# Edge softmax of a graph layer: indirect gathers spaced by clearings on GpSimd in place of waits on TensorE

## The chip, the core and the metric

The kernel runs on one core of a Trainium2 chip. The metric is device time in microseconds of one execution. Engines are named as in the profile: PE is TensorE (matmuls; PEld its weight loads), DVE is VectorE, ACT is ScalarE, POOL is GpSimd, SP is SyncE, which here only issues DMAs.

## The reference, cut to what matters

The kernel is a whole model of four layers on 16384 tokens of 64 channels. The change touches one stage of the third layer's feed-forward part: a graph attention over 262144 edges (and a loop at each node) that yields gate scores for four experts.

```python
h = (x_flat @ W_gat).reshape(M, HEADS, NUM_EXPERTS)        # M = 16384 nodes, 4 heads, 4 experts
a_src = (h * att_src).sum(-1)
a_dst = (h * att_dst).sum(-1)
e = leaky_relu(a_src[src] + a_dst[dst], negative_slope=0.2)
e_max = segment_max(e, dst, num_segments=M)
ee = jnp.exp(e - e_max[dst])
denom = segment_sum(ee, dst, num_segments=M)
alpha = ee / (denom[dst] + 1e-16)
msg = h[src] * alpha[:, :, None]
agg = segment_sum(msg, dst, num_segments=M).reshape(M, 16) + b_gat
```

What costs time in it is `h[src]` and `a_src[src]`: for each edge the row of its source node, 16 values and 4 logits.

## The kernel before, in words

The edges are sorted by destination and lie as 128 lanes of 2048 edges. `edge_softmax` (L3266) goes over them in 32 chunks of 64 columns; a column is 128 edges, one per lane. The source rows of the 64 columns of a chunk come in two ways:

- **34 columns by DMA** (`BY_DMA`): GpSimd issues one indirect gather per column (L3373), which reads 128 rows of 20 words from a table in HBM into `rows[:, k, c]`. `rows` is double: chunk n uses slot k = n mod 2.
- **30 columns on TensorE** (`ON_PE`, six groups of five): SyncE loads node places (`lanes`, L3326), VectorE compares them with node numbers to make one-hot matrices (`hot`, L3482, four instructions per group), TensorE multiplies these with the node table in two parts (L3391, eight matmuls of 128x512 per column into one of five PSUM banks), ScalarE copies each bank out (L3412), and VectorE picks one of 32 rows by the low bits of the number (`select`, L3497 to L3504).

VectorE then works through a chunk c: `logits` (L3510 to L3522), `maxima` (L3527 to L3539), `sums` (L3543 to L3548); ScalarE does the exponentials and turns the results round for the store. The order on VectorE is written out: during the six groups of chunk c+1 it does `logits(c)` behind group 0, `maxima(c)` behind group 1 and `sums(c)` at group 3.

What orders the gathers of chunk n:

- `idx_ready`: the column indices of chunk n are copied by VectorE in `maxima(n-2)` (L3468), behind its wait for the gathers of chunk n-2.
- `rows_used`: `sums(n-2)` (L3546) has read slot k for the last time. The first two chunks find both set ahead.
- `bank_full`, the pacing: gather c of chunk n waits until TensorE has filled a number of columns, `banks_before + c * ON_PE // BY_DMA`, so that 34 gathers go along with 30 columns. In the loop `banks_before` is `n * ON_PE - PACE_BEHIND`, ten columns early. The first two chunks stand ahead of the loop, with numbers of their own. Only c = 0 has no such wait.

The reader of the gathers of chunk n is `maxima(n)`: a wait on `gathered[k]` at L3527, behind which come L3468 (not in the last two chunks), L3531 and L3533. `wait_apart` (L36) is a wait followed by an increment of a semaphore that nobody waits for.

Of the kernel before, what the change touches and what calls it, by code (L numbers as in the profile page):

```python
# [10 lines left out]
BF16 = mybir.dt.bfloat16  # L11
# [8 lines left out]
P = 128  # L20
# [15 lines left out]
def wait_apart(eng, sem, value, passed):  # L36


    eng.wait_ge(sem, value)
    eng.sem_inc(passed, 1)  # L40
# [2855 lines left out]
HEADS2, CH = 4, 16  # L2896
# [170 lines left out]
GROUPS, PER_GROUP = 6, 5  # L3067
ON_PE = GROUPS * PER_GROUP
BY_DMA = CHUNK - ON_PE
# [2 lines left out]
LOW_PLACES = TILES // BLOCKS  # L3072
LOW_BITS = LOW_PLACES.bit_length() - 1
HOT_COLUMNS = CHUNKS * ON_PE
PACE_BEHIND = 2 * PER_GROUP


class HotPlaces:
# [187 lines left out]
def edge_softmax(nc, g, q, att_src):  # L3266

    C, W = CHUNK, CHUNK + 1
    NI = CHUNKS // 2
# [4 lines left out]
    with Stage(nc, "edges") as st:  # L3274
# [1 line left out]
        idx = st.sb("idx", [P, 2, C], I32)  # L3276
        inp_s, acc_s, decay = (st.sb(n, [P, HEADS2, 1 + PERH, W]) for n in ("inp_s", "acc_s", "decay"))
        lanes = st.sb("lanes", [P, LANE_SLOTS, PER_GROUP, P], F16)
        att = st.sb("att", [P, CH])
        nodes_i, nodes = st.sb("nodes_i", [P, BLOCKS], I32), st.sb("nodes", [P, BLOCKS])  # L3280
        pow2 = st.sb("pow2", [P, LOW_BITS], I32)
        tabs_p, weights_p, dst_p = (st.ps(n, [P, 512]) for n in ("tabs_p", "weights_p", "dst_p"))
# [22 lines left out]
        (split, numbered, powers, att_in, hot_ready, bank_full, fetched_in, halved, selected, pe_passed, act_passed, dve_passed, bits_ready) = (  # L3305
            st.sem(n) for n in ("split", "numbered", "powers", "att_in", "hot_ready", "bank_full", "fetched_in", "halved", "selected",
                                "pe_passed", "act_passed", "dve_passed", "bits_ready"))
        cleared, own, idx_ready, rows_used, passed, diff_ready, exped, sums_ready, state_ready, starts_used = (
            st.sem(n) for n in ("cleared", "vec_own", "idx_ready", "rows_used", "pool_passed", "diff_ready", "exped",
                                "sums_ready", "state_ready", "starts_used"))  # L3310
# [2 lines left out]
        with nc.Block() as block:  # L3313
# [47 lines left out]
            @block.gpsimd  # L3361
            def _(pool):
                nc.gpsimd.iota(nodes_i[:], pattern=[[1, BLOCKS]], base=0, channel_multiplier=BLOCKS).then_inc(numbered, 1)
                for s in range(LOW_BITS):
                    nc.gpsimd.memset(pow2[:, s:s + 1], LOW >> (s + 1)).then_inc(powers, 1)

                def gather(n, k, banks_before):
                    pool.wait_ge(idx_ready, n + 1)
                    wait_apart(pool, rows_used, n + 1, passed)
                    for c in range(BY_DMA):  # L3370
                        if c:
                            wait_apart(pool, bank_full, banks_before + c * ON_PE // BY_DMA, passed)
                        nc.gpsimd.indirect_dma_start(  # L3373
                            out=rows[:, k, c, :], out_offset=None, in_=q.t_table,
                            in_offset=bass.IndirectOffsetOnAxis(ap=idx[:, k, c:c + 1], axis=0)).then_inc(gathered[k], 16)

                gather(0, 0, 1)
                gather(1, 1, ON_PE - 4)
                with pool.Fori(1, NI) as i:
                    for k in range(2):  # L3380
                        gather(2 * i + k, k, (2 * i + k) * ON_PE - PACE_BEHIND)

            @block.tensor
            def _(pe):
# [415 lines left out]
def ffn2(nc, g, q, I):  # L3800

    turned_norm(nc, g, "ln_f2", g.H, known=True)
    with Stage(nc, "expc_in") as kept:
        tables = ExpertTables(nc, kept, I["L2_ffn_W1"], I["L2_ffn_W2"], I["L2_ffn_b1"], I["L2_ffn_b2"])
        with ExitStack() as ctx:
            q.tables(nc, ctx)
            node_logits(nc, g, q, I["L2_ffn_W_gat"], I["L2_ffn_att_src"], I["L2_ffn_att_dst"])
            edge_softmax(nc, g, q, I["L2_ffn_att_src"])
            carry_states(nc, g, q)
            node_gates(nc, g, q, I["L2_ffn_b_gat"], I["L2_ffn_ln_gamma"], I["L2_ffn_ln_beta"], ahead=tables)  # L3810
        experts(nc, g, "expc", tables, target=g.H, measure=True)
# [70 lines left out]
```

## Time and profile before

| | us |
|---|---|
| median of 3 runs | 6534.55 |
| lowest and highest run | 6527.07, 6545.31 |
| the profiled execution's own time | 6565.2 |
| its span | 6563.5 |
| edge stage in it, first gather to last store's issue | 3166.73 to 5022.19 |

| busy over the whole span | us |
|---|---|
| PE | 5217.5 (79%) |
| DVE | 4890.5 (75%) |
| ACT | 2537.8 (39%) |
| POOL | 2268.8 (35%) |

How to read it. The page is one profiled execution. A group of instructions has a line number, an engine, an operation, what it writes and reads and with which shapes, then its busy time and the mean of one in ns, then the idle time of the engine just before these instructions and what released it; "issue" means that the engine waited for nothing that the profile shows. In a timeline each row is start, duration, engine, line and operation, "x4" for four merged instructions, and in brackets the idle time before it. The table by stage gives for each stretch the busy time of each engine with its number of instructions, the granted clock of TensorE as a share of full speed, and the DMA engines' busy share. Times on POOL are rough: the duration of a gather is that of making its descriptors, not of its data's arrival.

### The profile page before, as it was taken

To read this page: it belongs to the slowest core of one execution; us is meant where nothing else is said; L and a number is where in the kernel's file an instruction comes from. 1 tells how busy PE (TensorE), PEld (TensorE's weight loads), DVE (VectorE), ACT (ScalarE), POOL (GpSimd) and SP (SyncE) were. 2 spreads that over 40 slices of the span, in tenths; PEclk is the share of its full clock that TensorE was granted. 3 is DMA by queue.
4 is the path that set the end of the run, shared out by engine and by line. 5 is a ranking of instruction groups with operands and counts; after the bars stand their busy time and mean duration, and the time that the engine had idled before them with its cause. 6 is when DMAs were issued, how large, how long until landed. Compare 5 with 4: busy or idle time off the path is not lost. (4 is left out here: it accounts for less than half of the span.)

```text
span 6563.5 us, 111024 instructions
## 1 busy us (share of the span) xinstructions
PE 5217.5 (79%) x41117; PEld 3540.3 (54%) x41184; DVE 4890.5 (75%) x8592; ACT 2537.8 (39%) x4432; POOL 2268.8 (35%) x2268
## 2 busy tenths in 40 slices
PE   6577968885469999971699999999994088967998
PEld 3462236554246666541577877778773025852452
DVE  6878988887878888870478888888886357767657
ACT  3443433333246666650233343333432043222332
POOL 0010010002223333325566666656663601014555
PEclk8778989997679999985799999999997598978999
DMA  0200000112210000001111121111111000030241
GB/s 17 78 6 1 20 23 29 35 41 65 72 32 6 6 9 11 10 10 40 22 39 40 37 41 41 41 36 41 40 40 27 8 1 3 3 65 15 68 105 33
DMA packets 241447, 206.47 MB, mean 31 GB/s; under 512 B 116682, under 2 KB 215923, under 8 KB 239251
## 3 DMA queue, kind: packets, MB, share of 16 engines
q1 hardware_dynamic: 173630, 147.27, 7.8%
q0 software_dynamic: 67408, 53.34, 5.3%
q8 instruction: 271, 4.44, 0.3%
q14 instruction: 126, 1.03, 0.1%
q10 hardware_dynamic: 12, 0.39, 0.0%
HBM read 113.55 MB, written 67.86 MB: 28 GB/s over the span
## 5 line engine op out<-in xcount | busy, mean ns | idle before, releaser
L3391 PE MATMUL edges_bank<-part_room,hot_room 128*128 128x512 f32 x7680 | 1778.8, 392 | 237.2 <-DVE hot_room L3482 190.0
L3391 PEld LDWEIGHTS edges_bank<-part_room,hot_room 128*128 128x128 f32 x7680 | 1440.3, 188 | 575.7 <-issue 253.6
L3373 POOL DMA_INDIRECT XT<-gat_node_table,edges_idx x1088 | 1113.8, 1024 | 706.4 <-issue 327.8
L3412 ACT COPY XT<-edges_bank 128x512 f32<-128x512 f32 x960 | 527.4, 605 | 1071.6 <-PE edges_bank L3391 695.3
L3500 DVE COPY_PREDICATED XT<-edges_tabs_p,XT 128x1280 f32<-128x1280 int32 (+3 forms) x768 | 648.3, 844 | 37.6 <-DVE edges_acc_s L3548 7.3
L3482 DVE TENSOR_SCALAR hot_room<-edges_lanes,edges_nodes 128x640 fp32r<-128x640 f16 x768 | 394.4, 576 | 298.8 <-PE edges_bank L3391 134.6
L1791 ACT ACTIVATE GT<-attc_sc,attc_nm 128x256 f32<-128x256 f32 x1024 | 399.8, 481 | 42.5 <-DVE attc_nm L1857 42.5
L1805 ACT ACTIVATE GT<-attc_sct 128x1024 f32<-128x1024 f32 x256 | 262.3, 1025 | 330.7 <-PE attc_sct L1725 329.7
L1856 DVE TENSOR_REDUCE attc_mx<-attc_sc 128x4 f32<-128x1024 f32 x256 | 313.3, 1224 | 89.3 <-PE attc_sc L1714 88.2
L1714 PE MATMUL attc_sc<-XT,attc_tT 64*128 64x256 f32 x2048 | 295.3, 407 | 52.5 <-ACT GT L1791 49.8
L505 POOL TENSOR_TENSOR X<-H,ln_f_mean 128x1024 f32<-128x1024 f32 x5 | 11.4, 2279 | 912.3 <-DVE ln_f_shift L542 912.3
L1861 DVE TENSOR_REDUCE attc_rs<-GT 128x4 f32<-128x1024 f32 x256 | 310.3, 1212 | 1.3 <-ACT GT L1791 1.2
L1735 PE MATMUL attc_op<-GT,attc_xB 128*64 128x256 f32 x2048 | 277.6, 391 | 10.3 <-ACT GT L1812 5.6
L1725 PE MATMUL attc_sct<-attc_tT,XT 64*128 64x256 f32 x2048 | 268.0, 379 | 1.7 <-DMA attc_tT<-attc_rT 1.0
L1714 PEld LDWEIGHTS attc_sc<-XT,attc_tT 64*128 64x128 f32 x2048 | 184.4, 189 | 151.9 <-issue 119.0
L2861 POOL DMA_INDIRECT X<-gat_samples,order_index x128 | 121.7, 951 | 334.8 <-PE attc_sc L1714 325.0
L2097 ACT ACTIVATE X<-attb_r 128x2048 f32<-128x2048 f32 x64 | 120.1, 1877 | 268.9 <-PE attb_r L2054 268.9
L2861 POOL DMA_INDIRECT X<-gat_blocks,order_index x128 | 121.3, 947 | 293.3 <-PE attc_sc L1714 281.2
L1725 PEld LDWEIGHTS attc_sct<-attc_tT,XT 64*128 64x128 f32 x2048 | 204.6, 188 | 22.2 <-ACT GT L1805 2.9
L786 PE MATMUL gates_gt<-identb,GT 128*128 128x128 bf16 x64 | 6.2, 263 | 263.0 <-DVE GT L777 261.5
L2393 DVE TENSOR_TENSOR X<-attd_r,attd_decay 128x2048 f32<-128x2048 f32 x64 | 146.6, 2291 | 81.9 <-PE attd_r L2296 81.9
L1735 PEld LDWEIGHTS attc_op<-GT,attc_xB 128*64 128x64 f32 x2048 | 129.6, 136 | 131.5 <-issue 97.5
(836 smaller groups left out, 10114.2 us busy)
## 6 DMA issues: line engine op xcount, KB each, us to landing
edges_lanes<-gat_places SPq DMA_DIRECT2D x192, 160.0 KB
gat_states<-GT SPq DMA_DIRECT2D x32, 768.0 KB
XT<-gat_node_table,edges_idx POOLq DMA_INDIRECT x1088
expert_pairs<-in_L_ffn_W_dram SPq DMA_DIRECT2D x48, 256.0 KB
XT<-XT SPq DMA_DIRECT2D x32, 256.0 KB
XT<-XT SPq DMA_DIRECT2D x64, 128.0 KB
XT<-XT SPq DMA_DIRECT2D x128, 64.0 KB
sorted_in<-stats SPq DMA_DIRECT2D x1, 5056.0 KB
```

The costliest lines, as they stand in the source:

```text
L1714: m = nc.tensor.matmul(sc[(0, 1, 1, 0)[hp]][:, n, a * S:(a + 1) * S], tT[half, b % NB, hp, a * P:(a + 1) * P], x(b, half), start=True, sto ...
L1725: m = nc.tensor.matmul(sct[:, n, j * S:(j + 1) * S], x(b, half)[:, j * P:(j + 1) * P], tT[half, b % NB, hp, :], start=True, stop=True)
L1735: m = nc.tensor.matmul(op[half, 0:S], xB[:, b % NB, j, (2 * hp + n) * D:(2 * hp + n + 1) * D], probT[:, hp % 2, n, j, :], start=hp + j == ...
L1791: m = nc.scalar.activation(prob[:, hp % 2, n, a, :], sc[(0, 1, 1, 0)[hp]][:, n, a * S:(a + 1) * S], ACT.Exp, bias=nm[:, b % 2, n, hp, a:a ...
L1805: nc.scalar.activation(probT[:, hp % 2].rearrange("p n j s -> p n (j s)"), sct[:], ACT.Exp, scale=scale).then_inc(probT_ready, 1)
L1856: link(vec.tensor_reduce(best, sc[(0, 1, 1, 0)[hp]][:].rearrange("p n (a s) -> p n a s", s=S), AX.X, ALU.max))
L1861: vec.reduce_sum(rs[:, b % 2, :, hp, :], prob[:, hp % 2], AX.X).then_inc(totaled, 1)
L3373: nc.gpsimd.indirect_dma_start(out=rows[:, k, c, :], out_offset=None, in_=q.t_table, in_offset=bass.IndirectOffsetOnAxis(ap=idx[:, k, c:c ...
L3391: m = nc.tensor.matmul(banks[t % BANKS][:], hot[:, (k * GROUPS + j) % 2, b, t, :], parts[:, p, b].rearrange("p u c -> p (u c)"), start=b = ...
L3412: nc.scalar.copy(fetched[:, (k * GROUPS + j) % 2, t].rearrange("p u c -> p (u c)"), banks[t % BANKS][:]).then_inc(fetched_in, 1)
L3482: m = vec.tensor_scalar(hot[:, (k * GROUPS + j) % 2, b], lanes[:, j % LANE_SLOTS], nodes[:, b:b + 1], None, ALU.is_equal)
L3500: vec.copy_predicated(half(0, w), taken(s, w), half(w, 2 * w)).then_inc(halved, 1)
```

## The change

A spare tile of 384 bf16 words in each lane is allocated (`spacer`). Behind each gather GpSimd clears it with a memset, and the gathers' waits on TensorE's columns are gone. The memset increments a new semaphore `spaced`; ahead of each memset stands a wait for the memset before it (`spaced` starts at 1). The waits on `idx_ready` and `rows_used` stay. The first two chunks are no longer written out ahead of the loop; the loop runs over all 16 pairs of chunks.

```diff
-PACE_BEHIND = 2 * PER_GROUP
+SPACER = 384
...
-        att = st.sb("att", [P, CH])
+        att, spacer = st.sb("att", [P, CH]), st.sb("spacer", [P, SPACER], BF16)
...
+        spaced = st.sem("spaced")
...
-                def gather(n, k, banks_before):
+                pool.sem_inc(spaced, 1)
+
+                def gather(n, k):
                     pool.wait_ge(idx_ready, n + 1)
                     wait_apart(pool, rows_used, n + 1, passed)
                     for c in range(BY_DMA):
-                        if c:
-                            wait_apart(pool, bank_full, banks_before + c * ON_PE // BY_DMA, passed)
                         nc.gpsimd.indirect_dma_start(
                             out=rows[:, k, c, :], out_offset=None, in_=q.t_table,
                             in_offset=bass.IndirectOffsetOnAxis(ap=idx[:, k, c:c + 1], axis=0)).then_inc(gathered[k], 16)
-
-                gather(0, 0, 1)
-                gather(1, 1, ON_PE - 4)
-                with pool.Fori(1, NI) as i:
+                        wait_apart(pool, spaced, n * BY_DMA + c + 1, passed)
+                        nc.gpsimd.memset(spacer[:], 0.0).then_inc(spaced, 1)
+
+                with pool.Fori(0, NI) as i:
                     for k in range(2):
-                        gather(2 * i + k, k, (2 * i + k) * ON_PE - PACE_BEHIND)
+                        gather(2 * i + k, k)
```

## Rows read from the trace of the kernel before

**Rows 1.** The page: costliest groups, the two of the edge stage.

```profile
L3391 PE MATMUL edges_bank<-part_room,hot_room 128*128 128x512 f32 x7680 | 1778.8, 392 | 237.2 <-DVE hot_room L3482 190.0
L3373 POOL DMA_INDIRECT XT<-gat_node_table,edges_idx x1088 | 1113.8, 1024 | 706.4 <-issue 327.8
```

**Rows 2.** Table by stage: the stage's first 20 us and 400 us of its middle.

```profile
core 0: us, PE busy (x) PEld busy (x) DVE busy (x) ACT busy (x) POOL busy (x), PEclk, DMA share, GB/s
3160.00:3180.00 20.00, 5.82 (x14) 4.57 (x15) 10.12 (x30) 0.59 (x1) 3.40 (x10) 0.50 0.27 56
...
4000.00:4400.00 400.00, 391.79 (x1699) 317.33 (x1698) 328.19 (x569) 158.01 (x260) 245.06 (x240) 1.00 0.19 39
```

**Rows 3.** Groups of instructions by line, stretch 3240 to 4950 us.

```profile
L3391 PE MATMUL edges_bank<-part_room,hot_room 128*128 128x512 f32 x7189 | 1663.7, 391 | 46.9 <-issue 33.5 <-ACT XT L3412 11.2 <-DVE hot_room L3482 0.6
...
L3482 DVE TENSOR_SCALAR hot_room<-edges_lanes,edges_nodes 128x640 fp32r<-128x640 f16 x716 | 368.0, 576 | 266.0 <-PE edges_bank L3391 108.3 <-DMA edges_lanes<-gat_places 75.3 <-DMA gat_dst_table<-gat_a_dst 68.4
```

**Rows 4.** Who waited for whom, same stretch: total us, times, longest.

```profile
POOL XT L3373 <- PE edges_bank L3391: 284.1, 136, 6.2
...
DVE hot_room L3482 <- PE edges_bank L3391: 108.3, 30, 7.8
```

**Rows 5.** Timeline: scan and first gathers of a chunk, 4022 to 4031 us.

```profile
start us, us, engine line op out<-in xcount [idle before <-releaser]
...
4025.25 2.87 DVE L3548 TENSOR_TENSOR_SCAN edges_acc_s<-edges_decay,edges_inp_s 128x1300 f32<-128x1300 f32 x1
4025.99 2.88 POOL L3373 DMA_INDIRECT XT<-gat_node_table,edges_idx  x1 [4.29 <-issue]
...
4029.17 0.95 POOL L3373 DMA_INDIRECT XT<-gat_node_table,edges_idx  x1 [0.30 <-issue]
```

**Rows 6.** Timeline of POOL, 4000 to 4060 us: gathers beside L3482.

```profile
4005.70 1.27 POOL L3373 DMA_INDIRECT XT<-gat_node_table,edges_idx  x1 [0.30 <-issue]
...
4050.95 1.11 POOL L3373 DMA_INDIRECT XT<-gat_node_table,edges_idx  x1 [0.30 <-issue]
```

**Rows 7.** Line L3373 by itself: least, median and greatest duration in ns.

```profile
L3373 POOL DMA_INDIRECT XT<-gat_node_table,edges_idx x1088: 938/944/3431, 3166.7 to 4984.9; - x182
```

**Rows 8.** Timeline of POOL, another stage: operation behind gather, gather behind operation.

```profile
2221.47 0.94 POOL L2861 DMA_INDIRECT X<-gat_samples,order_index  x1 [2.01 <-PE attc_sc L1714]
2222.42 1.07 POOL L2872 TENSOR_TENSOR X<-X,order_node 128x512 f32<-128x512 f32 x1
...
2052.91 1.02 POOL L2861 DMA_INDIRECT X<-gat_samples,order_index  x1 [0.47 <-POOL order_block L2878]
```

**Rows 9.** Timeline of POOL, early stages: memsets.

```profile
3.05 0.42 POOL L166 MEMSET embed_eg<- 128x384 f32 x1 [0.88 <-POOLq L82]
3.41 0.51 POOL L167 MEMSET embed_sel<- 6x512 bf16 x1
...
472.69 0.52 POOL L829 MEMSET expa_in_pick<- 128x512 f32 x1
```

**Rows 10.** Table by stage for L3482 alone, over the edge stage.

```profile
3166.70:5010.00 1843.30, 394.35 (x768) 0.99 0.19 39
```

**Rows 11.** Timeline: start of the stage, sums of chunk 0, end.

```profile
3165.32 0.13 POOL L3363 IOTA edges_nodes_i<- 128x4 int32 x1 [3.92 <-POOLq L82]
...
3166.73 1.08 POOL L3373 DMA_INDIRECT XT<-gat_node_table,edges_idx  x1 [1.14 <-DVE edges_idx L3468]
...
3277.94 2.27 DVE L3546 TENSOR_TENSOR edges_inp_s<-XT,edges_weights_p 128x1024 f32<-128x1024 f32 x1
...
4984.91 0.95 POOL L3373 DMA_INDIRECT XT<-gat_node_table,edges_idx  x1 [0.30 <-issue]
...
5008.41 0.17 DVE L3531 COPY stats<-stats 128x4 f32<-128x4 f32 x1
...
5022.19 0.35 SPq L3345 DMA_DIRECT2D gat_states<-GT  x1
```

## The prediction

> **What bounds the kernel now.** I read the page's costliest groups first [rows 1]: the 7680 matmuls of L3391 head them, and the 1088 indirect gathers of L3373 are GpSimd's largest group; both are the edge stage. Then the table by stage [rows 2]: in a stretch of 400 us in its middle TensorE is busy for 391.79 us, VectorE for 328.19, GpSimd for 245.06, at a granted clock of 1.00 (the 2.4 GHz level). So TensorE bounds the stage, with about 2% of idle time. One chunk is 240 matmuls; 1699 matmuls in 400 us make 56.5 us a chunk. The groups of the stage [rows 3] say the same: TensorE idles 46.9 us in 1710 us, and its main releaser is "issue", not a gather. In the table of waits [rows 4] I looked for L3468 and L3531, VectorE's first instructions behind its wait for a chunk's gathers. Neither has a row; VectorE's longest entry is L3482 on TensorE. So the gathers are hidden today. GpSimd's own waits on TensorE are the pacing that the change takes out: 284.1 us in this window.
>
> The question is therefore one of throughput: today 34 gathers fit into a chunk's 56.5 us with slack; do 34 gathers and 34 clearings fit?
>
> **The change part by part.**
>
> *Waits on TensorE's columns taken out.* They cost GpSimd idle time only. Without them the gathers run at their own pace. Worth 0 on the path by itself: nobody waits for a gather [rows 4].
>
> *One clearing behind each gather.* GpSimd works in order, so each gather now has the clearing of the gather before it ahead of it. The wait on the new semaphore is on the clearing before this one, which ended before the gather started, so it never stalls. Queued behind this wait on GpSimd are only clearings and gathers; who waits for them is VectorE's L3468 (L3531 in the last chunk), up to two chunks later.
>
> Cost of one pair, from rows:
> - Gather to gather: 1.25 us from start to start in a burst: 0.30 idle and 0.94 busy, as at 4029.17, where the one before had been held for 2.88 us and this one had long been due [rows 5]. The median of all 1088 is 0.944 busy [rows 7].
> - From a gather's end to a following GpSimd operation: 0.01 us (2221.47 + 0.94 to 2222.42) [rows 8].
> - The clearing: a memset of 128x384 f32 stands in the trace. It is reported at 0.42 us, but the next memset starts 0.36 us after it (3.05 to 3.41) [rows 9]. The tile is bf16; a memset of 512 bf16 elements takes 0.51 us and one of 512 f32 takes 0.52 us [rows 9], so the type changes nothing: it is the number of elements that counts. I take 0.36 and keep 0.42 as the upper end.
> - From the clearing's end to the next gather: the trace has no such pair without a wait between them. Nearest are the gather behind an operation with a wait on it, 0.47 us [rows 8], and the gather behind a gather, 0.30 us [rows 5]. Since another operation can start 0.01 us behind a gather, the 0.30 us belongs to the gather that comes and not to the one that went. I take 0.30, which is already in the 1.25. The lower end is 0: that it is passed while the clearing runs.
>
> The sum of one pair: 1.25 + 0.01 + 0.36 = 1.62 us. For 1088 pairs that is 1762.6 us.
>
> *Contention with VectorE.* The gathers' busy time is 1113.8 us [rows 1], against 1088 x 0.944 = 1027.1, so they are held up for 86.7 us today. Two rows show by what: the first gather of a chunk falls into the scan L3548 and takes 2.88 us in place of 0.94, some 30 times, [rows 5], and a gather beside L3482 takes 1.27 or 1.11 us [rows 6]. Both stay: add 86.7. The clearings meet L3482 too. It is busy 394.35 us of 1843.30, 21% [rows 10], so 228 of 1088 clearings start inside one. Held to its end they would wait half of its 0.5 us each, 57 us in all; not held at all, 0. I take the half, 28 us, since a gather beside L3482 is held up sometimes and sometimes not.
>
> Here the Trainium skill speaks against the change: the page SBUF — State Buffer, section "Who interferes with whom", says that VectorE in a 2-port mode and GpSimd share one port pair as an exclusive lock, held for the whole instruction. The gathers beside L3482 agree that there is a conflict [rows 6]; whether it lasts the whole instruction no row here shows. By that rule the full 57 us would stand in place of 28, and the sum below would come out 29 us higher.
>
> Sum: 1762.6 + 86.7 + 28 = **1877 us** of unbroken GpSimd work, 58.7 us a chunk against 56.5 of TensorE. GpSimd becomes the longer one.
>
> *How much of it is hidden.* The first gather starts at 3166.73 [rows 11]. The last chunk's gathers are needed by L3531 and L3533, which ran at 5008.41 [rows 11], right behind the last selection. I allow 2 us for the landing: an estimate between 0 and the 3.92 us that GpSimd idles between a last gather and the next stage's first operation [rows 11]. So 5008.4 - 2 - 3166.7 = **1839.7 us** are free, or 1.69 us a pair. Does anything stop GpSimd from using them without a break? A gather for chunk n waits until the sums of chunk n-2 are made. For n = 2 that is L3546, 3277.94 + 2.27 = 3280.2 [rows 11], while GpSimd would reach it at 3166.7 + 68 x 1.72 = 3283.7; after that it runs ever later than VectorE. So no. And the slack of middle chunks is large: gathers for a chunk start in the middle of the chunk two before it, so the lateness shows only near the end, as VectorE waiting at L3468 and L3531 in the last few chunks.
>
> Over: 1877 - 1840 = **+37 us**. The last gather would start near 5043 in place of 4984.91, and what follows (13.8 us from L3531 to the last store's issue [rows 11]) moves with it. The stages behind don't change. The profiled execution would go from 6565.2 (span 6563.5) to about 6602. The median of the runs shown, 6534.55, lies 30.65 below the profiled time; I add the 37 to the median: **6572 us**.
>
> *Ends of that sum.* Upper: the clearing at its reported 0.42 (+65) and the lock in full (+29): +131. Lower: no contention of the clearings gives +9, and and 0.01 us a pair less than that gives 0, since below 1.69 us a pair TensorE bounds the stage again.
>
> The Trainium skill's page Perfetto Trace Analysis, section "GPSIMD Engine Instruction", says to time GpSimd operations by the spacing of their starts and to distrust their reported durations. Here spacing gives 0.36 and the duration 0.42, and by the duration the sum would be 37 + 65 = +102 us; the trace decides for neither, as the row is a single pair of memsets.
>
> The new tile and semaphore cost nothing that a row shows: the stage has the same other tiles, and one more increment ahead of the loop. The first two chunks' gathers, which stood outside the loop, go into it: 2 of 32.
>
> **The rivals.**
>
> *A. The clearing hides in the gather's lead (not slower).* If the 0.30 us ahead of a gather passes while the clearing runs, a pair is 1.25 + 0.01 + 0.36 - 0.30 = 1.32 us. A chunk is then 34 x 1.32 + 2.7 + 0.9 = 48.5 us (the 2.7 and 0.9 are the 86.7 and 28 us over 32 chunks), under 56.5, and nothing on the path has changed. It decides from 1.69 us a pair downwards. For it: my sum, 1877 / 1088 = 1.725 us, is only 0.035 us from that point. Against it: the constant 0.30 us even where the next gather had long been due [rows 5], and 0.47 behind an operation [rows 8]. Price 0: 6535 us.
>
> *B. Even spacing helps TensorE (faster).* TensorE's idle time in the window is 46.9 us [rows 3], over half of it "issue", and gathers stand in bursts at 1.25 us [rows 5]. If these bursts delay what TensorE needs and GpSimd keeps up, up to 47 us come back; I price half, 24 us: 6511. It needs A's condition too. Against it: VectorE's and ScalarE's waits are fed by the same 160 KB loads in both kernels, and the mean rate of gathers stays.
>
> *C. The spacing isn't one.* The clearing is queued ahead of no wait that can hold. If GpSimd's parts run it beside the descriptors, gathers go at 1.25 to 1.32 us in a run of 34 and then stop until the sums. A chunk is 34 x 1.3 = 44 us of them, hidden as in A. 6535 us.
>
> *D. VectorE's waits reach TensorE's clock.* At the end VectorE waits at L3533, TensorE idles, and the clock may fall from 1.00 to 0.50, as it stood at the start of the stage, where 14 matmuls took 5.82 us, 0.42 each, against 391.79 / 1699 = 0.23 [rows 2]. Some 100 of them at 0.42 are 19 us on top of 37: 6591.
>
> **How the numbers follow.** The forecast (GpSimd is the bound, +5 to +131) has 0.57, A 0.20, C 0.06, B 0.12, D 0.05. The likeliest is the forecast at 6572. The range goes from 6515 (most of B inside) to 6650 (the upper end less the corner where both worst prices meet). What a measurement of this kernel can tell from no change is about 0.3%, 20 us. Slower by over that: 0.57 x 0.85 + 0.05 = 0.53. Faster: most of B, 0.10. Within: 0.37, from A, C and the low part of the forecast. The forecast's own range is 6540 to 6665.
>
> **What would show it.** The spacing of gathers in a run: 1.62 us free of contention if right, 1.32 if A, 1.25 if C. GpSimd busy or in its 0.30 leads without a break from 3167 to the stage's end, no wait of GpSimd on L3546, and the last gather near 5043. A wait of VectorE (L3468, L3531) on the gather's landing in the last five or so chunks, and none in the middle ones. L3482's mean, 576 ns now [rows 3], up by some tens of ns. The forecast is wrong if the gathers' idle time still shows a stop each chunk; its size is wrong if the pair isn't 1.62 or the excess over 0.944 isn't near 87 us.

## The result

The changed kernel takes 6548.36 us (median of 8 runs, 6537.3 to 6558.87) against 6534.47 (8 runs) of the kernel before: a ratio of 1.0025, 95% interval 1.0016 to 1.0034. It is 14 us slower, a quarter of a per cent. The prediction said 6572, 37 us slower, with GpSimd as the bound. The direction was right and GpSimd was indeed the bound; the size was not: the pair of gather and clearing was priced at 1.62 us and takes 1.55. TensorE gained something in between that the prediction gave to a rival.

The page of the changed kernel, the groups that answer to [rows 1], and two that the prediction spoke of. Lines are one higher than before in this stage.

```profile
L3392 PE MATMUL edges_bank<-part_room,hot_room 128*128 128x512 f32 x7680 | 1756.7, 390 | 237.8 <-DVE hot_room L3483 191.4
...
L3374 POOL DMA_INDIRECT XT<-gat_node_table,edges_idx x1088 | 1109.3, 1020 | 186.6 <-POOL edges_spacer L3378 173.4
...
L3483 DVE TENSOR_SCALAR hot_room<-edges_lanes,edges_nodes 128x640 fp32r<-128x640 f16 x768 | 503.3, 715 | 120.1 <-DMA edges_lanes<-gat_places 84.0
L3378 POOL MEMSET edges_spacer<- 128x384 bf16 x1088 | 547.6, 503 | 0.6
```

GpSimd's idle time before gathers fell from 706.4 to 186.6 us, and nearly all that is left is a fixed 0.16 us behind a clearing: it works without a break. L3483 (before: L3482) went from 576 to 715 ns.

The table by stage, middle and late stretches (compare [rows 2]):

```profile
4000.00:4400.00 400.00, 392.31 (x1721) 321.70 (x1720) 364.66 (x575) 164.53 (x262) 357.50 (x469) 1.00 0.18 39
4400.00:4800.00 400.00, 384.56 (x1681) 314.15 (x1680) 355.74 (x560) 161.24 (x256) 361.82 (x475) 1.00 0.18 39
```

In the middle TensorE does 1721 matmuls in 400 us, 55.8 us a chunk, **faster** than before (1699, 56.5). In the last third it does 1681, 57.1 us a chunk.

The groups in the stretch 3240 to 4950 us, as in [rows 3], and the waits, as in [rows 4]:

```profile
L3392 PE MATMUL edges_bank<-part_room,hot_room 128*128 128x512 f32 x7288 | 1665.5, 390 | 45.1 <-ACT XT L3413 45.1
```

```profile
POOL XT L3374 <- POOL edges_spacer L3378: 160.9, 1002, 0.2
...
DVE edges_idx L3469 <- DMA XT<-gat_node_table,edges_idx: 11.8, 8, 2.2
```

TensorE's idle time is as long as before, 45.1 against 46.9 us, but of another kind: "issue", 33.5 us of it before, is gone, and all of it is waiting for ScalarE to empty a bank. VectorE waits at L3469 for gathers 8 times, as forecast for the last chunks.

The timeline of POOL in the middle, and the end of the stage:

```profile
4165.35 0.95 POOL L3374 DMA_INDIRECT XT<-gat_node_table,edges_idx  x1 [0.16 <-POOL edges_spacer L3378]
4166.30 0.44 POOL L3378 MEMSET edges_spacer<- 128x384 bf16 x1
4166.90 0.95 POOL L3374 DMA_INDIRECT XT<-gat_node_table,edges_idx  x1 [0.16 <-POOL edges_spacer L3378]
4167.84 0.68 POOL L3378 MEMSET edges_spacer<- 128x384 bf16 x1
...
4986.68 0.95 POOL L3374 DMA_INDIRECT XT<-gat_node_table,edges_idx  x1 [0.16 <-POOL edges_spacer L3378]
...
4989.11 0.17 DVE L3532 COPY stats<-stats 128x4 f32<-128x4 f32 x1 [20.88 <-DMA XT<-gat_node_table,edges_idx]
...
5002.88 0.35 SPq L3346 DMA_DIRECT2D gat_states<-GT  x1
```

A pair that nothing holds takes 1.55 us from start to start (4165.35 to 4166.90). VectorE's L3532 waited 20.88 us for the last gather, and the stage ended 13.8 us after it, as in [rows 11]. This is the forecast's mechanism, seen whole.

The stage takes 1855 us from first gather to last store's issue in this profile, and 1855 in the profile of before that the prediction read. The second profile of the kernel before, below, shows why that is no tie: in the first the stage took 18 us longer than in the second.

### The profile page after: what moved, and what is told of

Same layout as the page of the kernel before. It is cut to its first block and busy times, and to the rows that moved or that the text cites. A ratio compares the mean times of both kernels' runs of the same rounds, so it can differ in the third digit from the quotient of the medians.

```text
span 6535.6 us, 112434 instructions
## 1 busy us (share of the span) xinstructions
PE 5177.7 (79%) x41184; PEld 3526.9 (54%) x41184; DVE 5032.8 (77%) x8592; ACT 2562.3 (39%) x4432; POOL 2816.1 (43%) x3356
## 5 line engine op out<-in xcount | busy, mean ns | idle before, releaser
L3392 PE MATMUL edges_bank<-part_room,hot_room 128*128 128x512 f32 x7680 | 1756.7, 390 | 237.8 <-DVE hot_room L3483 191.4
L3374 POOL DMA_INDIRECT XT<-gat_node_table,edges_idx x1088 | 1109.3, 1020 | 186.6 <-POOL edges_spacer L3378 173.4
L3413 ACT COPY XT<-edges_bank 128x512 f32<-128x512 f32 x960 | 544.4, 598 | 878.5 <-PE edges_bank L3392 639.2
L3483 DVE TENSOR_SCALAR hot_room<-edges_lanes,edges_nodes 128x640 fp32r<-128x640 f16 x768 | 503.3, 715 | 120.1 <-DMA edges_lanes<-gat_places 84.0
L3378 POOL MEMSET edges_spacer<- 128x384 bf16 x1088 | 547.6, 503 | 0.6
```

The lines of the kernel that those rows point to most:

```text
L3374: nc.gpsimd.indirect_dma_start(out=rows[:, k, c, :], out_offset=None, in_=q.t_table, in_offset=bass.IndirectOffsetOnAxis(ap=idx[:, k, c:c ...
L3378: nc.gpsimd.memset(spacer[:], 0.0).then_inc(spaced, 1)
L3392: m = nc.tensor.matmul(banks[t % BANKS][:], hot[:, (k * GROUPS + j) % 2, b, t, :], parts[:, p, b].rearrange("p u c -> p (u c)"), start=b = ...
L3413: nc.scalar.copy(fetched[:, (k * GROUPS + j) % 2, t].rearrange("p u c -> p (u c)"), banks[t % BANKS][:]).then_inc(fetched_in, 1)
L3483: m = vec.tensor_scalar(hot[:, (k * GROUPS + j) % 2, b], lanes[:, j % LANE_SLOTS], nodes[:, b:b + 1], None, ALU.is_equal)
```

## The experiments

All times are medians; each ratio is to the kernel before, measured alongside, whose medians were 6525.5 to 6526.0 us. Each edit is on the changed kernel unless said otherwise.

### Both kernels once more

> The changed kernel once more, to see what of the two profiles is the change and what is spread between executions. Theory T (GpSimd is the bound): gathers again 1.69 us apart on average, the chunk's gather starts 57.5 us apart, the stage from first gather to last store's issue 1855 +- 3 us; time 6548. If the change cost 14 us elsewhere, the stage stays at the 1855 of the kernel before and the 14 us show in another stage.

> The kernel before once more, for a second profile: its first one was 31 us over the median. If that was the stage, the stage is near 1840 us here against 1856; if it was other stages, the stage is again 1853 to 1858 and the 14 us by which the changed kernel is slower don't show in the profiles of the stage.

The changed kernel took 6536.62 us, ratio 1.0012 (1.0001 to 1.0023); that is 11 us, and 14 in the section above. The kernel before took 6529.27 in the one execution that was profiled again. In the second profiles the stages differ by 14 us:

| profile, us | first gather to first matmul | first to last matmul | last matmul to last store | stage |
|---|---|---|---|---|
| kernel before, second | 7.4 | 1808.2 | 21.8 | 1837 |
| changed kernel, second | 9.3 | 1799.2 | 42.8 | 1851 |

The kernel before, table by stage and its gathers and matmuls in the second profile:

```profile
4000.00:4400.00 400.00, 392.03 (x1706) 318.75 (x1705) 331.60 (x571) 162.03 (x264) 248.45 (x244) 1.00 0.18 41
```

```profile
L3391 PE MATMUL edges_bank<-part_room,hot_room 128*128 128x512 f32 x7266 | 1673.0, 390 | 37.5 <-issue 28.4 <-ACT XT L3412 6.8 <-DVE hot_room L3482 0.6
```

So the change makes TensorE's stretch 9 us shorter, starts it 2 us later and hangs 21 us on behind it, where everything waits for the last gathers. The stage's length is set by GpSimd: from the first gather to the end of the last one are 1836.1 us, and 15.2 us follow. The stages behind, which the change doesn't touch, took 1533 us in both profiles of the changed kernel and 1541 in both of the kernel before, so that the profiled executions differ by 7 us and not by 14. Why is open. Beneath the bound lie two larger effects on TensorE that nearly cancel; the next runs take them apart.

### Shorter clearings

```diff
-SPACER = 384
+SPACER = 320     # and 256
```

> The tile has 320 words in place of 384, nothing else. Theory T (GpSimd's pair of gather and clearing is the bound): the clearing is 64 words shorter, by the rows of 384 and 512 elements some 0.05 us, so a pair costs 1.64 us on average, a chunk 55.7 us, below TensorE's 56.0 of the first 22 chunks; the stage ends with TensorE near 1830 us, time about 6523 (25 under the changed kernel, 12 under the kernel before). Rival R (VectorE held up by the clearings is the cost): only a sixth of the clearing is gone, a sixth of the 14 us comes back, 6546.

> 256 words. Theory T: GpSimd 1.58 us a pair, 53.8 us a chunk, stops at each chunk until the sums; TensorE bounds, the same time as with 320 words within 5 us (6520). Rival R: a third of the 14 us comes back, 6543.

320 words: 6483.47 us, ratio 0.9926 (0.9913 to 0.9940). 256 words: 6457.12 us, ratio 0.9893 (0.9874 to 0.9912). Both beat both kernels. The gain is more than theory T had: 53 and 79 us under the changed kernel in place of 25. The 256 words:

```profile
4000.00:4400.00 400.00, 399.88 (x1762) 330.18 (x1761) 354.76 (x590) 168.82 (x268) 352.04 (x499) 1.00 0.18 41
```

```profile
L3392 PE MATMUL edges_bank<-part_room,hot_room 128*128 128x512 f32 x7308 | 1659.2, 389 | 0.9 <-ACT XT L3413 0.6
...
L3483 DVE TENSOR_SCALAR hot_room<-edges_lanes,edges_nodes 128x640 fp32r<-128x640 f16 x728 | 418.8, 635 | 134.7 <-DMA edges_lanes<-gat_places 74.4 <-PE edges_bank L3392 47.0 <-issue 9.0
...
L3503 DVE COPY XT<-XT 128x80 f32<-128x80 f32 x183 | 44.9, 245 | 6.2
```

TensorE is busy for 399.88 of 400 us, 1762 matmuls, 54.5 us a chunk, and idles 0.9 us in the whole window. T explains that the bound goes; it doesn't explain that the middle chunks, where GpSimd is awaited by nobody, went from 55.8 to 54.5 us. The theory was short of a part; the runs below show it to be the clearings' weight on VectorE.

### No clearing at all

```diff
-                        wait_apart(pool, spaced, n * BY_DMA + c + 1, passed)
-                        nc.gpsimd.memset(spacer[:], 0.0).then_inc(spaced, 1)
```

> The waits on TensorE's columns are gone and no clearing takes their place: gathers follow one another at 1.25 us, 34 of them, then a stop until the sums. TensorE's idle time with releaser 'issue' (33.5 us in the window before, 0 in the changed kernel) tells two theories apart. Theory B (bursts of gathers hold up what TensorE's sequencer needs): the idle time returns, 30 us or more, time at 6534 or above. Theory W (the waits on TensorE's columns caused it): it stays away, a chunk takes TensorE 55.6 to 56.0 us, the time is about 6510.

7393.82 us, ratio 1.1319 (1.1304 to 1.1335): 868 us slower than the kernel before. Theory B was right, and its "30 us or more" of idle time came to 643. TensorE's group, stretch 3240 to 5780 us:

```profile
L3390 PE MATMUL edges_bank<-part_room,hot_room 128*128 128x512 f32 x7387 | 1893.9, 410 | 648.3 <-issue 643.1
```

And a burst in the timeline. Its first gather, at 3993.49, was held by the scan; from 3996.68 on they follow at 1.25 us, and fifteen us later TensorE goes short:

```profile
4010.43 0.94 POOL L3374 DMA_INDIRECT XT<-gat_node_table,edges_idx  x1 [0.30 <-issue]
4011.38 0.19 PEld L3390 LDWEIGHTS edges_bank<-part_room,hot_room 128*128 128x128 f32 x1 [0.46 <-issue]
4011.68 0.94 POOL L3374 DMA_INDIRECT XT<-gat_node_table,edges_idx  x1 [0.30 <-issue]
4012.09 0.39 PE L3390 MATMUL edges_bank<-part_room,hot_room 128*128 128x512 f32 x1 [0.74 <-issue]
...
4014.88 0.45 PE L3390 MATMUL edges_bank<-part_room,hot_room 128*128 128x512 f32 x1 [1.71 <-issue]
```

From there on TensorE gets single matmuls, although the bank and the columns are there. Of the 507 distances over 0.6 us between the starts of two matmuls in this stage nine in ten lie within 0.06 us of a multiple of 0.70, mostly 0.7 to 3.5 us. In the stage's 31 bursts the shortage begins behind 13 to 16 gathers (once 22), and it ends 5 to 6 us behind the start of the last gather in most. Gathers at 1.25 us without a gap starve it; VectorE's and ScalarE's operations keep their durations. The table by stage for this kernel: the whole stage, the burst's first 13.3 us, and the starved stretch.

```profile
3151.00:5862.00 2711.00, 1976.16 (x7680) 1520.33 (x7680) 1478.07 (x2571) 740.14 (x1167) 1092.57 (x1088) 0.81 0.11 26
3996.70:4010.00 13.30, 13.30 (x60) 11.04 (x59) 9.05 (x16) 5.42 (x8) 10.25 (x11) 1.00 0.24 68
4011.00:4040.00 29.00, 8.03 (x16) 3.91 (x15) 5.76 (x10) 1.17 (x2) 20.35 (x22) 0.57 0.07 8
```

The granted clock falls with the idle time, to a mean of 0.57 in the starved stretch: there most matmuls take 0.59 us in place of 0.39. The stage is 873 us longer than in the second profile of before. TensorE is busy for 206 us of these (1976 against 1770, at a clock of 0.81 against 0.99): matmuls that stand alone don't overlap, and the clock is lower, which the runs don't split. The rest is idle time. The loading of instructions is not what is short, as far as the trace shows: the profile counts 271 and 125 packets of kind "instruction" over the execution here, 271 and 126 in the kernel before.

```profile
q8 instruction: 271, 4.44, 0.2%
q14 instruction: 125, 1.02, 0.0%
```

In the kernel before the same happens in small: it makes up lost time in bursts of ten and more gathers at 1.25 us after each scan, and 28 to 34 us of "issue" follow. In its second profile TensorE loses 1.5 us a chunk at columns 3 and 4, which stand 12 to 13 gathers behind the scan.

### How slow the gathers must be

```diff
-SPACER = 384
+SPACER = 192     # and 64
```

> 192 words, a gather each 1.39 us when nothing holds it. TensorE has nothing left to win over 256 words (54.5 us a chunk is 240 matmuls at 0.227 us). So the same time within 5 us if gathers at this pace don't starve TensorE yet; higher if they do, since at 1.25 us they do from some twelve gathers on.

> 64 words, a gather each 1.28 us: nearly the pace of the unspaced kernel (1.25). If TensorE's starving is a matter of the gathers' rate near a limit, idle time with releaser 'issue' returns in part or in full, between 6500 and 7400. If anything between two gathers is enough, the time stays at 6457.

192 words: 6646.97 us, ratio 1.0179 (1.0152 to 1.0206). 64 words: 7295.48 us, ratio 1.1185 (1.1168 to 1.1202). With 192 words TensorE's "issue" idle time is back:

```profile
L3392 PE MATMUL edges_bank<-part_room,hot_room 128*128 128x512 f32 x7228 | 1720.0, 396 | 90.6 <-issue 70.8 <-ACT XT L3413 15.1 <-DVE hot_room L3483 0.9
```

The first gap comes 26 to 36 gathers into a run. The window in which this works is narrow: a gather each 1.44 us (256 words) starves nobody, each 1.39 us (192) costs 190 us against it.

### One clearing for two gathers

```diff
-SPACER = 384
+SPACER = 512
...
-                        wait_apart(pool, spaced, n * BY_DMA + c + 1, passed)
-                        nc.gpsimd.memset(spacer[:], 0.0).then_inc(spaced, 1)
+                        if c % 2:
+                            wait_apart(pool, spaced, n * (BY_DMA // 2) + c // 2 + 1, passed)
+                            nc.gpsimd.memset(spacer[:], 0.0).then_inc(spaced, 1)
```

> A clearing of 512 words behind every second gather in place of one of 256 behind each: pairs at 1.25 us, then 1.6 us, the same mean of 1.44 us when nothing holds them. If TensorE's starving goes by the mean rate over some ten gathers, this is as good as the 256 words, 6457 within 10 us. If it goes by the distance of one gather to the next, half of them are at 1.25 and the time rises by 50 us or more.

6481.59 us, ratio 0.9935 (0.9918 to 0.9953), 24 us over the 256 words: between the two theories' numbers, nearer to the mean rate. TensorE idles 7.2 us for "issue" and 5.8 for ScalarE in the window 3240 to 4900. So it is mainly the rate over many gathers that counts, not the distance of one to the next. The longer clearings have a weight of their own here, and the 24 us are not split between the two.

### The waits kept, the clearing added

The kernel before, with

```diff
+SPACER = 256
...
                             wait_apart(pool, bank_full, banks_before + c * ON_PE // BY_DMA, passed)
                         nc.gpsimd.indirect_dma_start(
...
+                        wait_apart(pool, spaced, n * BY_DMA + c + 1, passed)
+                        nc.gpsimd.memset(spacer[:], 0.0).then_inc(spaced, 1)
```

> The kernel before with its waits on TensorE's columns kept, and a clearing of 256 words behind each gather added. If the waits cost nothing by themselves and the kernel before loses its time to bursts of gathers that starve TensorE, the clearings break the bursts: idle time with releaser 'issue' goes from 33.5 us to near 0, TensorE near 54.5 us a chunk, time within 10 us of 6457. If the waits themselves cost time, 6500 or more.

6473.6 us, ratio 0.9917 (0.9899 to 0.9935). That is 16 us over the 256 words alone, outside the 10 of the expectation, but mostly not in this stage: first to last matmul takes 1746.2 us in its profile against 1745.5, and TensorE idles 0.9 us in the window in both. Of the 18 us between the two profiles 13 lie ahead of the stage, and why is open; 4 lie at the stage's end, where the last gather starts at 4921.7, 9 us behind the last matmul. Along TensorE's stretch the waits cost nothing; what the clearing gives is the missing gap in the bursts. Against the kernel before the clearings alone, with the waits as they were, take TensorE's stretch from 1808.2 to 1746.2 us.

### Spacing without a clearing

```diff
-                        wait_apart(pool, spaced, n * BY_DMA + c + 1, passed)
-                        nc.gpsimd.memset(spacer[:], 0.0).then_inc(spaced, 1)
+                        for m in range(13):
+                            pool.sem_inc(idle[m % 2], 1)
```

> In place of each clearing GpSimd's sequencer does 13 increments of semaphores that nobody reads, at 0.078 us each by the trace: gathers come at about 1.55 us as in the changed kernel, but nothing writes to SBUF between them. Theory L (the clearings hold up VectorE's L3482 and L3502, the scan of the sums ends 1.6 us later in each chunk, ScalarE's copies behind it too, and TensorE waits for a bank at column 26): L3482 back at 575 ns, TensorE at 54.5 us a chunk, time within 10 us of the one with 256 words, 6460. Rival P (the pace alone decides, 1.55 us being too slow): 56 us a chunk and 6530 as in the changed kernel.

6571.27 us, ratio 1.0073 (1.0057 to 1.0088): neither number. The time was forecast wrong because GpSimd's sequencer doesn't keep the pace: gathers came 1.48 us apart mostly, but 1.717 on average, in this kernel's profile. Why it doesn't is open. The increments make GpSimd's loop longer, and the profile counts more packets of instructions on queue 14, 266 in place of 126, but only about a fifth of the distances over 2 us between two gathers have such a packet in them:

```profile
q14 instruction: 266, 2.18, 0.1%
```

That makes it a second test of the bound: 1088 x 1.717 = 1868 us of gathers, 32 more than in the changed kernel's second profile (1836), and a time 35 us longer. The chunks before the lateness shows are the test of theory L, stretch 3260 to 3640 us, this kernel first, the changed kernel below:

```profile
3260.00:3640.00 380.00, 380.00 (x1678) 314.67 (x1677) 326.41 (x561) 161.70 (x256) 225.74 (x219) 1.00 0.19 42
```

```profile
3260.00:3640.00 380.00, 371.88 (x1630) 304.81 (x1629) 344.30 (x548) 156.01 (x247) 340.70 (x450) 1.00 0.19 40
```

Without writes between the gathers TensorE is never idle, 54.4 us a chunk, at a pace of gathers of 1.75 us on average in this stretch against the changed kernel's 1.69, and L3484 (L3483 in the changed kernel) is back at 583 ns. With the clearings a chunk takes 56.0. So the pace isn't what costs these 1.6 us a chunk, the clearings are.

### Clearings behind 30 of 34 gathers

```diff
-                        wait_apart(pool, spaced, n * BY_DMA + c + 1, passed)
-                        nc.gpsimd.memset(spacer[:], 0.0).then_inc(spaced, 1)
+                        if c < ON_PE:
+                            wait_apart(pool, spaced, n * ON_PE + c + 1, passed)
+                            nc.gpsimd.memset(spacer[:], 0.0).then_inc(spaced, 1)
```

> 384 words, but the last four gathers of each chunk have no clearing. GpSimd's work falls by 4 x 0.46 us to 55.7 us a chunk, so it isn't the bound at the end of the stage; the clearings beside VectorE are nearly as many. If the changed kernel pays for both (lock and bound), this one keeps TensorE's 56.0 us a chunk for all chunks and loses the last gather's lateness: 20 to 25 us under the changed kernel. If the bound costs nothing, it stays within 5 us. If the lock costs nothing, TensorE is at 54.5 and the time near 6460.

6513.18 us, ratio 0.9979 (0.9970 to 0.9989), 23 us under the changed kernel, as expected if the bound is one limit and the clearings' weight another one beneath it. Its groups in the stretch 3240 to 4900 us:

```profile
L3393 PE MATMUL edges_bank<-part_room,hot_room 128*128 128x512 f32 x7117 | 1625.9, 390 | 34.6 <-ACT XT L3414 33.1 <-DVE hot_room L3484 1.4
```

A chunk takes TensorE 56.0 us on average from beginning to end of the stage, and the gathers are in time. Taking away the bound is worth 23 us; then the clearings' weight on VectorE is the limit. This kernel is 56 us over the 256 words, and in the profiles 45 of them are TensorE's stretch, 1791 us against 1746.

### How the clearings reach TensorE

The changed kernel's timeline at the sums of a chunk:

```profile
4197.54 2.41 DVE L3483 TENSOR_SCALAR hot_room<-edges_lanes,edges_nodes 128x640 fp32r<-128x640 f16 x4
...
4198.90 0.70 POOL L3378 MEMSET edges_spacer<- 128x384 bf16 x1
...
4208.33 2.87 DVE L3549 TENSOR_TENSOR_SCAN edges_acc_s<-edges_decay,edges_inp_s 128x1300 f32<-128x1300 f32 x1
...
4211.23 2.74 ACT L3431 COPY GT<-edges_acc_s 128x1024 f32<-128x1024 f32 x1 [5.97 <-DVE edges_acc_s L3549]
4213.69 1.68 ACT L3413 COPY XT<-edges_bank 128x512 f32<-128x512 f32 x3
4214.45 3.74 PE L3392 MATMUL edges_bank<-part_room,hot_room 128*128 128x512 f32 x15 [0.75 <-ACT XT L3413]
```

ScalarE takes L3431 ahead of L3413, as written. It waits 5.97 us for VectorE's scan, then copies sums for 2.74 us, and only then empties banks; TensorE, with five banks, has run out of them. That chain stands in the kernel before too, with 11.2 us lost in [rows 3]. The clearings push it over the edge: L3483 takes 715 ns in place of 576, the small copy L3503 some 400 in place of 212, and the scan ends later. Averages of chunks 2 to 21, counted from 0 (the copy's over TensorE's whole stretch):

| kernel | mean of the small copy, ns | scan's end behind the chunk's first matmul, us | TensorE's loss at columns 26 and 27, us | a chunk, us |
|---|---|---|---|---|
| 384 words | 396 | 47.1 | 1.4 | 55.9 |
| 384 words, 30 of 34 | 386 | 47.1 | 1.3 | 56.0 |
| 512 words, each second | 365 | 46.3 | 0.8 | 55.2 |
| 320 words | 289 | 46.0 | 0.4 | 54.9 |
| 256 words | 244 | 45.5 | under 0.1 | 54.5 |

The loss goes with the scan's end. (In the kernel before the scan ends at 47.5 us, but there TensorE is late itself, by the 1.5 us of columns 3 and 4 among others, and loses only 0.2 us here.) It doesn't go with the mean of L3483 alone, which is 690 ns with 30 of 34 clearings and 696 with 320 words.

## Why the prediction was right and wrong

**What bounds the kernel before: half right.** TensorE does, and the gathers are hidden. But I read its 2% of idle time as nothing to be had, and 33.5 us of "issue" as no business of the gathers. Bursts of gathers cause it. Rival B named exactly this and was given 0.12; its price of 24 us was too low: with the waits kept and 256 words added TensorE's stretch is 62 us shorter. I argued against it from the mean rate of gathers, which stays; it is the rate within a burst that matters, and rows 5 showed such a burst. In the changed kernel B happened, "issue" went to 0, but that couldn't shorten the time, since GpSimd was longer.

**The pair: two terms wrong, against each other. This is the step that failed.** Predicted 1.25 + 0.01 + 0.36 = 1.62 us; measured 0.95 + 0.44 + 0.16 = 1.55. Over 1088 pairs that is some 80 us too much.
- The lead of a gather was 0.16 us behind a clearing, not 0.30. The rule I drew, that the 0.30 belongs to the gather that comes, doesn't hold: -0.14 x 1088 = -152 us. My bounds of 0 and 0.30 held it.
- The clearing counts with its full 0.44 us, not with 0.36: the overlap seen between two memsets isn't there before a gather. About +71 us with the 0.01. Here the page Perfetto Trace Analysis of the Trainium skill, "GPSIMD Engine Instruction", had advised the spacing of starts; that advice was sound only for the pair of operations whose spacing it was. The spacing to the operation that really follows is what has to be measured, and no row of before had it.

**Contention of the gathers: right.** 87 us carried over; 1109.3 - 1088 x 0.951 is 75, or 82 against the old 0.944.

**Contention of the clearings: too small, and one side of it forgotten.** Their mean is 503 ns against a median of 437: 1088 x 0.066 = 72 us, where I took 28 and had 57 as the upper end:

```profile
L3378 POOL MEMSET edges_spacer<- x1088: 432/437/775, 3149.1 to 4987.6; 128x384 bf16 x182
```

The rule of the Trainium skill's page SBUF — State Buffer, "Who interferes with whom", an exclusive lock for the whole instruction, was the better guide; the trace agrees with its full price and more. That is 72 us against 57. I also used it only for what VectorE does to GpSimd. The other direction, GpSimd to VectorE, stood in my list of signs ("L3482's mean up by some tens of ns") and in no term of the sum. It was 139 ns up. In the changed kernel's own time this is hidden: TensorE's stretch ends 27 us before the last gather does (4958.8 against 4986.1 in the second profile). It is the next limit beneath: 45 us of TensorE's stretch between clear_30_of_34 and the 256 words.

**The sum of GpSimd's work:** 1877 predicted, 1840 and 1836 in the two profiles. **The free time:** 1840 predicted from the first profile of before. By the second one, L3531 at 4972.67 and the first gather at 3148.96 leave 4972.7 - 2 - 3149.0 = 1822. Over: 1836 - 1822 = 14 us, which is what the stage grew by in the second profiles. So the shape of the sum was sound; the work was 40 us too large and the free time 18 us too large, and the difference of two large numbers kept their errors. That the medians of the first measurement differ by 14 us as well is in part luck: the second pair differs by 11, and the stages behind, which the prediction left as they were, differ by 8 us the other way in the profiles. The profiled execution stood 31 us above the median and above all eight runs, and I moved the result by that constant without asking where it had lost the time. Of the 36 us by which it exceeds the second profile, 18 lie in the stage and 18 ahead of it.

**The rivals.** A (the lead is hidden): half of the lead was. C (the spacing isn't one): wrong, pairs are spaced exactly. D (the clock falls): the granted clock is 1.00 from 4800 to 4960 us too, up to the last matmul, because VectorE's long wait comes only when TensorE is done. "Nobody waits for a gather, so the waits taken out are worth 0" was right for the waits (waits_and_256), but only because something else does their second job: without waits and without clearings the kernel is 13% slower.

**What the change is worth, put together.** Against the 54.5 us a chunk that TensorE can do, the kernel before loses 2 us a chunk, most of it to bursts of gathers. The changed kernel wins nearly all of that back and loses 1.5 us a chunk to the clearings' weight on VectorE: 9 us are left of the gain in TensorE's stretch. Its stage ends with the gathers all the same, and 23 us (2 ahead of the first matmul, 21 behind the last) stand against the 9. The 14 us that remain are the stage's part; the medians say 11 to 14 for the whole.

## What to carry to other kernels

A spacer has a window: it must be long enough for what the bursts disturb, and short enough that the spaced work fits its period and its own contention fits the slack of the others; here 384 words are over both limits, 320 at their edge, 256 inside, 192 under, and one size tried on either side would have shown it. When an engine idles for "issue", look at what other engines' queues do in the 15 us before it, at their rate in a burst and not on average. And before a difference of two near-equal sums is trusted, get a second profile of the same kernel.

## What was not expected of the hardware

- A long run of indirect gathers on GpSimd starves TensorE of whatever stands behind "issue": at 1.25 us a gather from behind 13 to 16 gathers on, with 64 words between them (1.28 us) still nearly as badly, at 1.39 us late in each run of 34, at 1.44 us never. The matmuls then mostly come at multiples of 0.70 us. The durations of the gathers don't change (0.94 us), the DMA engines are busy for 11% of that stage and for 24% in the burst before the shortage, and no more instructions are loaded than before. What is short was not found.
- Behind a memset a gather starts after 0.16 us, behind a gather after 0.30, and a memset behind a gather after 0.00.
- A clearing costs 0.33, 0.38 and 0.44 us for 256, 320 and 384 words, in bf16, by the medians: some 0.11 us and 0.84 ns a word.
- A gather that starts inside the scan L3549 (2.87 us) ends some 0.75 us behind the scan's end: 3993.49 to 3996.37 in the unspaced kernel, 2.88 us in place of 0.94. Beside L3547, also with two inputs, gathers keep 0.94 us.
- Thirteen semaphore increments of the sequencer space gathers by 1.48 us in most cases, but not steadily.
